# Products with 64x64 node matrices as one 128x128 block-diagonal product, or as four 64x64 products on the quarters of TensorE's array

## The reference

```python
# layer 2: U are the eigenvectors of the normalized Laplacian (64x64)
agg = einsum('mn,bnd->bmd', U.T, h)
out = relu(agg @ W1 + b1) @ W2 + b2
x = x + einsum('nm,bmd->bnd', U, out)
# layer 3: S = adj * adj (64x64)
h = relu(S @ (h @ W1))     # 128 -> 256 features
h = relu(S @ (h @ W2))     # 256 -> 512
x = x + S @ (h @ W3)       # 512 -> 128
```

## Time and profile before

| | us |
|---|---|
| median of the runs | 953.56 |
| the profiled execution, its own time | 955.17 |
| its span, first to last instruction | 953.4 |
| TensorE busy | 849.2 (89%) |
| VectorE busy | 564.5 (59%) |
| ScalarE busy | 517.3 (54%) |
| GpSimd busy | 315.7 (33%) |
| mean granted TensorE clock | 0.968 of full |

### The profile page before, as it was taken

One profiled execution on the slowest core, in us unless ns is written; L12 is line 12 of the kernel. 1 busy time (PEld: TensorE's weight loads), 2 busy tenths in 40 slices (PEclk: granted clock), 3 DMA queues, 4 the chain that ended last, 5 costly groups with the idle time before them and its releaser, 6 DMA issues.

```text
span 953.4 us, 12338 instructions
## 1 busy us (share of the span) xinstructions
PE 849.2 (89%) x3723; PEld 558.3 (59%) x3723; DVE 564.5 (59%) x3050; ACT 517.3 (54%) x958; POOL 315.7 (33%) x373
## 2 busy tenths in 40 slices
PE   2777597798999889996899799988999999999998
PEld 1444344644687446863467545766568658858847
DVE  5899878799678977799886858436015005204101
ACT  1566585575656555664565455675364463454521
POOL 1333201375556544565564566004003002202000
PEclk9999898899999989998999899999999999999999
DMA  8000000000000000000000000000001000000101
GB/s 348 0 1 1 1 0 1 1 0 1 1 1 0 1 2 0 1 1 1 0 1 1 1 1 1 0 1 1 1 1 45 1 1 14 32 0 2 45 1 45
DMA packets 3395, 13.27 MB, mean 14 GB/s; under 512 B 512, under 2 KB 512, under 8 KB 2688
## 3 DMA queue, kind: packets, MB, share of 16 engines
q1 hardware_dynamic: 3328, 12.48, 3.3%
HBM read 8.28 MB, written 4.19 MB: 13 GB/s over the span
## 4 chain that ended last, share of the span: by engine, by line
PE 57%; DVE 14%; ACT 4%; POOL 2%; issue 1%; ACTq 0%; DVEq 0%
PE PS L455 56%; POOL BIG L1002 1%; ACT BIG L911 1%; DVE X L1878 1%; ACT T L877 1%; DVE Fq L1475 1%; DVE seg L1476 1%; ACT T L823 1%; PE PS L641 1%; DVE stats L1651 1%; DVE PS L1369 1%; DVE PS L1371 1%; DVE Z L1376 1%; DVE Z L1373 0%; ACT BIG L934 0%
## 5 line engine op out<-in xcount | busy, mean ns | idle before, releaser
L455 PE MATMUL PS<-BIG,wts 128*128 128x512 f32 (+2 forms) x952 | 341.3, 501 | 9.4 <-ACT BIG L911 7.0
L1002 POOL TENSOR_TENSOR BIG<-BIG 128x256 f32<-128x256 f32 (+2 forms) x220 | 211.0, 967 | 162.5 <-ACT BIG L911 96.2
L455 PEld LDWEIGHTS PS<-BIG,wts 128*128 128x128 f32 x952 | 177.4, 193 | 132.1 <-issue 95.9
L911 ACT ACTIVATE BIG<-PS,lbias 128x256 f32<-128x256 f32 (+2 forms) x312 | 162.6, 559 | 113.7 <-PE PS L455 111.6
L455 PE MATMUL PS<-H,wts 128*128 128x256 f32 (+2 forms) x312 | 115.0, 494 | 9.1 <-POOL H L1002 4.7
L815 ACT ACTIVATE BIG<-PS 128x1024 f32<-128x1024 f32 x64 | 65.5, 1023 | 88.5 <-PE PS L455 88.5
L815 ACT ACTIVATE T<-PS 128x512 f32<-128x512 f32 x96 | 55.7, 594 | 91.6 <-PE PS L455 91.3
L455 PE MATMUL PS<-T,wts 128*128 128x512 f32 x192 | 101.1, 648 | 1.7 <-ACT T L815 1.5
L1878 DVE TENSOR_TENSOR X<-X,PS 128x512 f32<-128x512 f32 x64 | 43.2, 679 | 99.3 <-PE PS L455 87.1
L979 POOL TENSOR_SCALAR rstd<-mv 128x4 f32<-128x4 f32 x48 | 11.0, 228 | 266.0 <-DVE mv L1679 266.0
L1925 DVE TENSOR_TENSOR T<-PS,wts 128x512 f32<-128x512 f32 x16 | 11.1, 691 | 142.9 <-PE PS L455 142.9
(11 more groups left out here) (318 smaller groups left out, 1194.9 us busy)
## 6 DMA issues: line engine op xcount, KB each, us to landing
X<-x_in SPq DMA_DIRECT2D x4, 1024.0 KB, 16.8
out<-X SPq DMA_DIRECT2D x16, 256.0 KB, 2.0
wts<-w_in SPq DMA_DIRECT2D x1, 3542.0 KB, 13.7
cst<-cst_in SPq DMA_DIRECT2D x1, 419.0 KB, 3.5
AA<-adj_in SPq DMA_DIRECT2D x2, 16.0 KB, 2.1
```

The lines of the kernel that those rows point to most:

```text
L455: return nc.tensor.matmul(o, l, r, start=start, stop=stop)
L911: nc.scalar.activation(LB[:, q, {"i": I_, "g": G_, "f": F_, "o": O_}[g], 0:n], PS[:, 3 * q + rank[q] % 3, 0:n], ACT.Tanh if g == "g" else ...
L1002: nc.gpsimd.tensor_tensor(out, a, b, op).then_inc(pool_set[q], 1)
```

## The change

Every product with a block-diagonal node matrix is taken apart. The matrices are 64x64 in each diagonal block, so each 128x128 product becomes four 64x64 ones (`graph_rows(g)` are the partitions of graph g of a tile), each on one quarter of the array: partitions of the operand choose the quarter's rows, partitions of the output its columns.

- `nodes_of_two` (agg, mix1) takes a pair of chunks: 32 products of 64x64 weights with 64 columns for the pair, in place of 8. For each tile and chunk the order is: graph 0 and graph 1 into like halves of the partitions, then both into the other halves. Results of graph g of both chunks stand in bank 2(k + g).
- `nodes_of_hidden` (mix2): 32 products of 64 columns per chunk in place of 8; graph g in bank 2k + g. ScalarE's copy reads the banks in another order (`by_graph`).
- `back_of_two` (back, mix3): four products with 64x64 weights and 512 columns for a pair of chunks in place of two.
- The results of agg and mix1 are copied out by two engines: ScalarE takes the columns of graph 0, VectorE those of graph 1 (`graph_half`, `other_half`; 256 columns each). The product behind (w1, s1) waits for both halves of both chunks of the pair.

```diff
--- before.py
+++ after.py
@@ -155,7 +155,7 @@
                begun=["agg", "turn_h"])
 D_ACT = d_order(C_ACT.end, ["aggT", "hid"], ["s3"], ["norm3", "mix1T", "relu1", "mix2T", "relu2a", "relu2b"],
                 ["norm"])
-D_DVE = d_order(C_DVE.end, ["o", "add"] + [s + "3" for s in LN], ["add3"], [], LN, ["add_h"])
+D_DVE = d_order(C_DVE.end, ["half", "o", "add"] + [s + "3" for s in LN], ["add3"], ["half3"], LN, ["add_h"])
 A_POOL = Steps(BEGUN, LNP)
 C_POOL = Order(A_POOL.end, [(0, n) for n in LNP + ["h"]])
 D_POOL = d_order(C_POOL.end, [s + "3" for s in LNP], [], [], LNP, first=False)
@@ -422,6 +422,20 @@
         def odd_bank(k):
             return PS[:, 2 * k + 1, :]
+        def graph_rows(g):
+            return slice(g * NODES, (g + 1) * NODES)
+        def graph_half(k, g):
+            odd = k % 2
+            there = PS[:, 2 * (k - odd + g), odd * 256:(odd + 1) * 256]
+            at = g ^ odd
+            return by_graph(T1[:, k, 0:CH])[:, :, at, :], there.rearrange("p (t n) -> p t n", t=TPC)
+        def by_graph(ap):
+            return ap.rearrange("p (t g n) -> p t g n", g=2, n=NODES)
         def begin(eng, *groups):
             for group in groups:
@@ -733,6 +747,41 @@
             pe.wait_ge(prep_dve, PREP["all"])
+            def back_of_two(k, weights, columns, out_bank):
+                for odd in range(2):
+                    for g in range(2):
+                        j = mm(out_bank(k + odd)[graph_rows(g ^ odd), :], weights[graph_rows(g), graph_rows(g)], T1[graph_rows(g), k + odd, columns])
+                    j.then_inc(pe_done[k + odd], 1)
+            def nodes_of_two(k, weights):
+                for n, (t, odd) in enumerate(itertools.product(range(TPC), range(2))):
+                    for cross in range(2):
+                        for g in range(2):
+                            f = g ^ cross
+                            a = odd * 256 + t * NODES
+                            j = mm(PS[graph_rows(f), 2 * (k + g), a:a + NODES],
+                                   T0[graph_rows(g), k + odd, t * P + f * NODES:t * P + (f + 1) * NODES], weights[graph_rows(g), graph_rows(g)])
+                            if n == 2 * TPC - 1 and cross and not g:
+                                j.then_inc(pe_done[k], 1)
+                j.then_inc(pe_done[k + 1], 1)
+            def nodes_of_hidden(k):
+                for t in range(TPC):
+                    for c in range(2):
+                        for cross in range(2):
+                            for g in range(2):
+                                f = g ^ cross
+                                a, b = (c * TPC + t) * NODES, t * 256 + c * P + f * NODES
+                                j = mm(PS[graph_rows(f), 2 * k + g, a:a + NODES], R1[graph_rows(g), k, b:b + NODES],
+                                       BDST[graph_rows(g), graph_rows(g)])
+                j.then_inc(pe_done[k], 1)
             def last_products(i):
                 for k in range(NK):
@@ -742,42 +791,50 @@
                             j = mm(banks(k)[:, 1, t * P:(t + 1) * P], R2[:, k, c * CH + t * P:c * CH + (t + 1) * P],
                                    W("l3w3")[:, c * P:(c + 1) * P], start=(c == 0), stop=(c == 3))
                     j.then_inc(pe_done[k], 1)
-                for k in range(NK):
-                    pe.wait_ge(act_done[k], D_ACT.at(i, "s3"))
-                    mm(banks(k)[:, 1, :], BDST[:, :], T1[:, k, CH:2 * CH]).then_inc(pe_done[k], 1)
+                for k in range(0, NK, 2):
+                    for c in (k, k + 1):
+                        pe.wait_ge(act_done[c], D_ACT.at(i, "s3"))
+                    back_of_two(k, BDST, slice(CH, 2 * CH), odd_bank)
             for i in range(ITER):
-                for k in range(NK):
-                    pe.wait_ge(act_done[k], D_ACT.at(i, "norm"))
-                    if i:
-                        pe.wait_ge(act_done[k], D_ACT.at(i - 1, "relu2b"))
-                    else:
+                for k in range(0, NK, 2):
+                    for c in (k, k + 1):
+                        pe.wait_ge(act_done[c], D_ACT.at(i, "norm"))
+                        if i:
+                            pe.wait_ge(act_done[c], D_ACT.at(i - 1, "relu2b"))
+                    if not i:
                         for q in range(2):
                             pe.wait_ge(act_set[q], R_ACT.start(ITER))
-                    tiles(bank(k), k, T0[:, k, :], BDU[:, :])
+                    nodes_of_two(k, BDU)
                 if i == 0:
                     pe.wait_ge(dve_done[NK - 1], C_DVE.end)
                     for k in range(NK):
                         product(ITER - 1, "turn_h", k, odd_bank(k))
                 for k in range(NK):
-                    pe.wait_ge(act_done[k], D_ACT.at(i, "aggT"))
+                    for c in (k, k ^ 1):
+                        pe.wait_ge(act_done[c], D_ACT.at(i, "aggT"))
+                        pe.wait_ge(dve_done[c], D_DVE.at(i, "half"))
                     mm(bank(k), W("l2w1"), T1[:, k, 0:CH]).then_inc(pe_done[k], 1)
                 for k in range(NK):
                     pe.wait_ge(act_done[k], D_ACT.at(i, "hid"))
                     tiles(bank(k), k, T0[:, k, :], W("l2w2"))
-                for k in range(NK):
-                    pe.wait_ge(dve_done[k], D_DVE.at(i, "o"))
-                    mm(bank(k), BDUT[:, :], T1[:, k, 0:CH]).then_inc(pe_done[k], 1)
+                for k in range(0, NK, 2):
+                    for c in (k, k + 1):
+                        pe.wait_ge(dve_done[c], D_DVE.at(i, "o"))
+                    back_of_two(k, BDUT, slice(0, CH), bank)
                 if i:
                     last_products(i - 1)
-                for k in range(NK):
-                    pe.wait_ge(act_done[k], D_ACT.at(i, "norm3"))
-                    tiles(bank(k), k, T0[:, k, :], BDST[:, :])
-                for k in range(NK):
-                    pe.wait_ge(act_done[k], D_ACT.at(i, "mix1T"))
+                for k in range(0, NK, 2):
+                    for c in (k, k + 1):
+                        pe.wait_ge(act_done[c], D_ACT.at(i, "norm3"))
+                    nodes_of_two(k, BDST)
+                for k in range(NK):
+                    for c in (k, k ^ 1):
+                        pe.wait_ge(act_done[c], D_ACT.at(i, "mix1T"))
+                        pe.wait_ge(dve_done[c], D_DVE.at(i, "half3"))
                     if i:
                         pe.wait_ge(dve_done[k], D_DVE.at(i - 1, "add3"))
@@ -789,11 +846,7 @@
                     j.then_inc(pe_done[k], 1)
                 for k in range(NK):
                     pe.wait_ge(act_done[k], D_ACT.at(i, "relu1"))
-                    for t in range(TPC):
-                        for c in range(2):
-                            j = mm(banks(k)[:, c, t * P:(t + 1) * P],
-                                   R1[:, k, t * 256 + c * P:t * 256 + (c + 1) * P], BDST[:, :])
-                    j.then_inc(pe_done[k], 1)
+                    nodes_of_hidden(k)
                 for half, before in ((0, "mix2T"), (1, "relu2a")):
                     for k in range(NK):
                         pe.wait_ge(act_done[k], D_ACT.at(i, before))
@@ -938,7 +991,8 @@
             for i in range(ITER):
                 for k in range(NK):
-                    copy(k, T1[:, k, 0:CH], bank(k), D_PE.at(i, "agg"))
+                    act.wait_ge(pe_done[k ^ 1], D_PE.at(i, "agg"))
+                    copy(k, *graph_half(k, 0), D_PE.at(i, "agg"))
                 for k in range(NK):
                     copy(k, T0[:, k, :], bank(k), D_PE.at(i, "w1"), ACT.Relu, bias=W("l2b1"))
                 for k in range(NK):
@@ -946,11 +1000,12 @@
                         copy(k, T1[:, k, CH:2 * CH], banks(k)[:, 1, :], D_PE.at(i - 1, "s3"))
                     norm_tiles(i, k, "norm3", D_DVE.at(i, "shift3"), D_PE.at(i, "w2"))
                 for k in range(NK):
-                    copy(k, T1[:, k, 0:CH], bank(k), D_PE.at(i, "mix1"))
+                    act.wait_ge(pe_done[k ^ 1], D_PE.at(i, "mix1"))
+                    copy(k, *graph_half(k, 0), D_PE.at(i, "mix1"))
                 for k in range(NK):
                     copy(k, R1[:, k, :], both(k), D_PE.at(i, "s1"), ACT.Relu)
                 for k in range(NK):
-                    copy(k, A2[:, k, :], both(k), D_PE.at(i, "mix2"))
+                    copy(k, by_graph(A2[:, k, :]), banks(k).rearrange("p g (t n) -> p t g n", n=NODES), D_PE.at(i, "mix2"))
                 for k in range(NK):
                     copy(k, R2[:, k, 0:1024], both(k), D_PE.at(i, "s2a"), ACT.Relu)
                 for k in range(NK):
@@ -1919,7 +1974,14 @@
             for k in range(NK):
                 add(ITER - 1, k, odd_bank(k), D_PE.at(0, "turn_h"))
+            def other_half(i, k, name):
+                for c in (k, k ^ 1):
+                    dve.wait_ge(pe_done[c], D_PE.at(i, name))
+                v.tensor_copy(*graph_half(k, 1)).then_inc(dve_done[k], 1)
             for i in range(ITER):
```

(4 more changed lines are left out.)

## The result

After the change the kernel takes **943.99 us**, median of four runs (943.46 to 945.46), against 953.62 before (953.52 to 959.08): ratio 0.9892, 95% interval 0.987 to 0.9914. It is faster by 1.1%; forecast were 970 us and slower. The profiled execution took 944.04 us, its span 942.3, so 11.1 less than before.

The account below looks back on a forecast made before the run. TensorE was taken as the bound in the last two layers behind their first 23 us. Terms 4.3 + 0 + 5.6 + 2.2 + 0.4 + 0.7 + 1 + 1.8 = 16.0 took 955.17 to 971.2, 970 us for the median; range 928 to 1000.

Parts of the forecast that it names:

- never more than two quarters work at once: TensorE's node products: in program order, a second record overlaps only the next product's first; 0.06 us small, 0.43 wide; chance 0.36.
- +4.3 and 0: Forecast change in TensorE product time, in us: +4.3 for 1024 small products, 0 for 64 wide ones.
- a floor of 0.03 per record: Second reason for 0.06 us per small product: if every record costs 0.03, two records cannot take less.
- all four quarters at work: Rival for TensorE's node products: all quarters overlap, products fall by 40.1 us, not all arriving; 935 us, chance 0.31.
- sum of -18.9: Net kernel change in us if all four quarters work, after shape changes, first iteration, agg, VectorE and clock.
- own term for it, +2.2: First iteration: the first l2w1 product starts 2.2 us later, waiting for two more VectorE copies at 0.4 each.
- the 1 that I set: First iteration: longer TensorE idle time brings a lower clock that hits mix1 and s1; +1 us, 0 to 3.
- 0.33 of the prediction: TensorE loses 0.33 us per burst of small products to array shape changes; 17 bursts, +5.6 us.
- agg in iterations 2 to 4: agg's second pair waits for chunk 3's normalisation, ending at 705.9 instead of 704.93; +0.6 us each, +1.8 together.
- the rival's 1.0 us per iteration: Before s1, VectorE's four additions and two half copies behind shorter mix3 and mix1 give back 3 x 1.0 us.
- serial loads: Rival: weight loads of different quarters do not overlap, +61 us, 1031 us; chance 0.21 together with nothing shared.
- a price of 0.03 per record: Rival: wide products shared by four quarters, small ones bound by 0.03 us per record; 959 us, chance 0.12.

Follow-up runs that it names:

- experiment 5: Kernel before the change with only mix2 on the quarters, each chunk's eight products for one quarter issued together before the next quarter's; 977.11 us, one run.
- experiment 8: Against the change: all products on quarters, but agg and mix1 chunk by chunk, copied by ScalarE alone, no pairs or half copies; 939.06 us.
- experiments 10 and 11: Kernel before the change with mix2, back and mix3 on quarters, agg and mix1 on the full array; mix2 in one burst 939.03 us, in two bursts 935.66.
- experiment 3: Kernel before the change with only agg and mix1 on the quarters, with pairs of chunks and VectorE's half copies; 957.33 us.
- kernel 9: experiment 8 with mix2 in two bursts, the last chunk's s1 and first chunk's s2a between them; 937.09 us.
- experiment 7: Kernel before the change with only mix2 on the quarters, and the first iteration's mix2 computed four times over; 971.88 us, one run.

## Why the prediction was wrong

**The bound** was read rightly: behind the first mix1 TensorE is the kernel, and what its products lost, the time lost, as far as it did not turn into a wait on TensorE.

**The step that failed** is the one between the bounds: "never more than two quarters work at once. A small product then costs one record, 0.06, a wide one 0.43". Measured are 3.89 / 128 = 0.030 us a small product and 1.96 / 8 = 0.245 a wide one. So the two terms of the sum, +4.3 and 0, should have been near -26 and -12 (1024 x 0.030 for 57.1, and 64 x 0.245 for 27.5). That alone turns the forecast round. The row about 64x64 products had two of them on the same quarter, and from one quarter nothing about the order among quarters can be read; I made a rule of it. The trace after shows first records of four products before any second one. Whether the engine takes them out of turn or gets them so, it does not show. That runs on one quarter cost 0.097 (experiment 5) says that turns are needed. That the time still lies in the stated range is no credit to the forecast: the range was drawn to hold this rival too. The second reason, a floor of 0.03 per record, is refuted as well: two records per product take 0.030 together.

**The rival "all four quarters at work"** had the mechanism, and mix2 of 3.9 us and back near 1.7 (1.96) as its marks; its 935 us was 9 too low. Against its sum of -18.9 the span shows -11.1, 7.8 short. By rows:
- waits for instructions, which had no term: 0.75 + 1.34 + 1.22 + 1.32 = 4.6 by their rows. From start to start it is more: the three mix2 bursts take 5.54, 5.33 and 5.52 us for 3.89, 4.7 longer, and mix1 of the second iteration 2.99 for some 1.95, 1.0 longer; together 5.7. The fifth, in the first agg, falls where the gain was counted as lost;
- the first iteration: it put the layer norms first and left out that VectorE's half copies move these too. The first `l2w1` product comes 2.6 us later (8.02 against 5.43 behind agg). The forecast's own term for it, +2.2, was near (a half copy takes 0.35 us, the term had 0.4);
- the half clock: TensorE stood idle for 6.8 us before mix1 instead of 3.15, and the windows (busy us of PE first, PEclk third from the end) show the level of 1.2 GHz until s1:

```profile
656.00:659.00 3.00, 0.00 (x0) 0.00 (x0) 2.90 (x17) 2.66 (x7) 1.99 (x3) 0.56 0.00 0
659.00:662.00 3.00, 1.99 (x64) 1.83 (x64) 1.16 (x8) 2.71 (x7) 1.27 (x2) 0.50 0.03 5
662.00:666.50 4.50, 3.83 (x69) 3.38 (x70) 1.68 (x9) 1.72 (x6) 0.00 (x0) 0.50 0.00 0
```

  s1 takes 8.07 us (664.59 to 672.66), before 6.91 (659.60 to 666.51); the second mix1 pair takes 1.92, an agg pair at the full clock 1.10. Less 0.2 for the shape that is 1.8, for the 1 that I set, within its bounds of 0 to 3;
- the earlier part, +1.24, not of the change;
- the other way, changes of shape: s2a behind mix2 takes 27.67 instead of 27.47 (701.12 less 673.65), s3 behind back 14.49 instead of 14.29. 0.2 per burst for the 0.33 of the prediction, so 3.4 for 5.6.

That is 5.7 + 2.6 + 0.8 + 1.2 - 2.2 = 8.1 for 7.8. It is not a closed account, for it leaves out terms that go both ways: VectorE before s1 costs 1.4 in all and not 3.0, agg ends 0.2 later each time and not level, a wide product of back costs 0.245 and not 0.215. By stretches, with the rival's own terms put where they belong, the code ahead of the stage is 1.2 of the 7.8, the first iteration 2.2, the three from s2a to s2a 4.4, and the end nothing.

**agg in iterations 2 to 4** goes from 704.22 to 708.23, 4.01 us, where it took 3.81. The forecast had its end 1.0 later (705.9 for 704.93, of which +0.6 were its own term), it is 0.2; the mechanism, a wait for chunk 3's normalisation, is there as 1.75 us `<-ACT T`. So in pairs a node product four times as fast wins nothing there; chunk by chunk (experiment 8) agg takes 3.34.

**VectorE before s1**: the rival's 1.0 us per iteration shows as 0.71 in the third and the fourth.

**The other rivals**, serial loads and a price of 0.03 per record, are out by the 3.89.

## What to carry to other kernels

Whether parts of an array work side by side is seen only in a trace that has two of them at once; a row with one of them gives the price of one and says nothing about sharing, and then the ends of the range deserve equal weight. When work is cut into many short instructions, count them too: here four quarters used 256 instructions in 1.95 us and one block of 256 arrived per 3.45 to 4.0, and splitting the burst with longer work in between brought it back (experiments 10 and 11). And a faster product in front of which another engine's result is awaited wins little, and nothing at the price of a copy on a third engine: agg went from 3.81 to 4.01 us in pairs and to 3.34 chunk by chunk. mix1, whose data are there in the later iterations, went from 3.57 to 2.34 (experiment 3) and 2.42 (experiment 8). Read such a gain iteration by iteration: in experiments 3 and 8 and in kernel 9 one bad iteration hides it in the total.

## What the runs showed that was not expected

- Four 64x64 fp32 products on four quarters, given in turn, take 0.12 us together, as one alone; given quarter by quarter, four take 0.39.
- A wait for instructions shows as `<-issue` inside a row of like matmuls. In experiment 7 it recurs each 256 instructions once the first 218 matmul records are through, with 1.3 to 1.9 us. In experiment 8 and kernel 9 such a wait, of 1.83 and 1.84 us, is followed by a granted clock of 0.50, which costs another 1.7 us.
- The end of the untouched first 634 us moved by 3.3 us between profiled executions (631.78 to 635.07), more than several of the effects here; comparing from the first row of the edited stage on took it out.
